# Diagonal attention on one core: rows of queries and keys turned by DMA transposes instead of TensorE transposes and bank copies

## What is computed

```python
Q = X_embed @ W_q + b_q
K = X_embed @ W_k + b_k
V = X_embed @ W_v + b_v
Q = (Q * scale).reshape(n, heads, l, d)      # 16 heads of 8 channels
K = (K * scale).reshape(n, heads, l, d)
V = V.reshape(n, heads, l, d)
scores = jnp.einsum('neax,nebx->neab', Q, K)
A = jax.nn.softmax(scores, axis=2)           # over the query axis
diag = jnp.diagonal(A, axis1=2, axis2=3)
out = (diag[..., None] * V).reshape(n, l, hid) @ W_o + b_o
```

## Time and profile before

| | before |
|---|---|
| median of three runs | 4593.46 us |
| the profiled execution's own time | 4590.25 us |
| its span | 4588.9 us |
| granted TensorE clock over the span | 0.81 of 2.4 GHz |
| busy: PE, PEld, DVE, ACT, POOL | 81%, 43%, 74%, 65%, 19% |
| phase F, first score to the close of the last tile | about 2502 to 3824 us |

### The profile page before, as it was taken

How to read it: one execution, slowest core, us unless ns; L and a number is a source line. 1 busy time by engine, 2 the same in 40 slices (tenths; PEclk the granted TensorE clock), 3 DMA queues, 4 the chain that set the end, 5 groups by cost and what they waited for, 6 DMA issues and landing times.

```text
span 4588.9 us, 77986 instructions
## 1 busy us (share of the span) xinstructions
PE 3731.4 (81%) x30870; PEld 1964.0 (43%) x30870; DVE 3378.4 (74%) x5283; ACT 2974.1 (65%) x4944; POOL 875.9 (19%) x1122
## 2 busy tenths in 40 slices
PE   6999778888599999899997566666666567899998
PEld 4666523232244445666665111111111113566666
DVE  6778676676320116777886999999999996778787
ACT  3655346656343435566665999999998996566665
POOL 2444301000076760000001122221122110000000
PEclk8999769989699999999998555555555558899999
DMA  1000000000311100000000000000000000000000
GB/s 46 1 1 1 3 0 1 1 1 1 89 33 41 37 12 20 7 10 11 2 2 8 1 0 1 1 1 1 1 1 1 5 1 19 6 11 4 9 2 20
DMA packets 51785, 47.38 MB, mean 10 GB/s; under 512 B 21827, under 2 KB 35790, under 8 KB 51406
## 3 DMA queue, kind: packets, MB, share of 16 engines
q1 hardware_dynamic: 51422, 42.39, 3.8%
HBM read 31.75 MB, written 2.23 MB: 7 GB/s over the span
## 4 chain that ended last, share of the span: by engine, by line
PE 43%; DVE 29%; issue 10%; ACT 7%; DMA 0%; POOL 0%; SPq 0%; DVEq 0%; ACTq 0%; POOLq 0%
DVE d_negmax L2728 14%; PE psum L2245 6%; PE psum L2274 6%; DVE f_m_E L2344 6%; PE psum L2260 5%; PE psum L1906 5%; PE psum L1929 5%; ACT d_junk L2793 3%; PE psum L1302 2%; PE psum L1291 2%; PE psum L1270 2%; DVE f_pT_E L2363 2%; DVE wl_negmax L1408 1%; ACT wl_p L1543 1%; PE psum L2651 1%
## 5 line engine op out<-in xcount | busy, mean ns | idle before, releaser
L2728 DVE TENSOR_REDUCE d_negmax<-psum 128x1 f32<-128x1024 f32 x1024 | 1183.5, 1212 | 57.1 <-PE psum L2651 56.0
L2793 ACT ACTIVATE d_junk<-psum,d_negmax 128x1024 bf16<-128x1024 f32 x1024 | 1136.4, 1118 | 108.3 <-DVE d_negmax L2728 100.4
L2651 PE MATMUL psum<-d_qT,d_kT 64*128 64x512 bf16 x2048 | 606.2, 601 | 487.6 <-ACT d_junk L2793 472.5
L2438 ACT ACTIVATE hidden<-psum,f_nm_E 128x1024 f32<-128x1024 f32 x512 | 566.4, 1113 | 144.3 <-DVE f_nm_E L2347 144.1
L2344 DVE TENSOR_REDUCE f_m_E<-psum 128x1 f32<-128x1024 f32 x512 | 601.8, 1217 | 47.4 <-PE psum L2245 46.2
L2245 PE MATMUL psum<-f_k_E,f_q_swapped_E 64*128 64x512 f32 x1024 | 526.5, 624 | 6.5 <-ACT hidden L2438 6.5
L2245 PE MATMUL psum<-f_k_E,f_q_E 64*128 64x512 f32 x1024 | 526.1, 623 | 3.2 <-DMA f_q_swapped_E<-f_q_E 1.2
L2445 ACT COPY f_pT_E<-psum 128x512 f32<-128x512 f32 x512 | 300.0, 586 | 321.3 <-PE psum L2260 321.2
L2274 PE MATMUL psum<-f_pT_E,f_v_E 128*64 128x128 f32 x8192 | 505.4, 276 | 2.5 <-DVE residual L2374 2.5
L2651 PEld LDWEIGHTS psum<-d_qT,d_kT 64*128 64x128 bf16 x2048 | 105.7, 101 | 925.7 <-ACT d_junk L2793 877.5
L2363 DVE COPY f_pT_E<-psum 128x512 f32<-128x512 f32 x512 | 351.4, 686 | 160.9 <-PE psum L2260 151.4
(11 more groups left out here) (344 smaller groups left out, 4945.5 us busy)
## 6 DMA issues: line engine op xcount, KB each, us to landing
moe_gates_on_all<-moe_gate_spill SPq DMA_DIRECT2D x8, 2048.0 KB, 14.1
f_q_swapped_E<-f_q_E SPq DMA_DIRECT2D x64, 128.0 KB, 2.3
moe_w<-in_moe_w SPq DMA_DIRECT2D x8, 256.0 KB, 4.3
out<-residual SPq DMA_DIRECT2D x1, 2048.0 KB, 8.7
residual<-in_hidden_states SPq DMA_DIRECT2D x2, 768.0 KB, 7.4
residual<-in_hidden_states SPq DMA_DIRECT2D x2, 256.0 KB, 3.1
m_taps<-in_m_conv SPq DMA_DIRECT2D x4, 128.0 KB
level_sums<-in_c_sums SPq DMA_DIRECT2D x1, 512.0 KB
```

Of the source, the lines that this page charges most:

```text
L2438: A.activation(pb[:, u % 2, f * 2 * BANK:(f + 1) * 2 * BANK], two(2 * f), ACT.Exp, bias=nm[:, u % 4:u % 4 + 1], scale=SC, accum_out=rs[:, ...
L2651: last = T.matmul(bank(2 + 2 * (at % 3) + jj), kT[half, s, jb * P:(jb + 1) * P], qT[half, s, hf * BANK:(hf + 1) * BANK], start=True, stop= ...
L2728: V.tensor_reduce(mh[:, t % 2, n // 2, n % 2:n % 2 + 1], two(2 + 2 * (at % 3)), X, ALU.max, negate=True).then_inc(*maxed.up(at))
L2793: A.activation(junk[:, at % 3, :], two(2 + 2 * (at % 3)), ACT.Exp, bias=mh[:, t % 2, n // 2, n % 2:n % 2 + 1], accum_out=sh[:, t % 2, n // ...
```

## The change

The three groups of transposes on PE, DVE's two copies and ACT's copy out of the side banks go. In their place SP issues two DMA transposes for each tile, from SBUF to SBUF: `d_q_rows` (128 x 1024 bf16, 256 KB) to `d_qT`, and `d_k_rows` (128 x 2048 bf16, 512 KB) to `d_kT`. A block of 128 x 128 now holds two sets of 64 rows: for the queries the two halves of the tile, for the keys the same keys twice. So `uq` keeps its size in another order, `uk` is twice as large, and POOL writes each with six copies in place of three. The keys' transpose waits for that of the queries to land; both wait for the spread copies, for the transposes of the tile before, and for the last use of the buffers that they overwrite. The loads of the chosen heads (`fr.sp_heads(0)`) now stand on SP behind the transposes of tile 30.

```diff
-                uq = sb(st, "d_q_rows", [P, 2, NH, len(TERMS), HD], BF16)
-                uk = sb(st, "d_k_rows", [P, 2, NH, len(TERMS), HD], BF16)
+                uq = sb(st, "d_q_rows", [P, 2, NH // 2, 2, len(TERMS), HD], BF16)
+                uk = sb(st, "d_k_rows", [P, 2, NH, 2, len(TERMS), HD], BF16)
...
-                    if t + 1 < R:
-                        side += [("rows", t + 1, k) for k in range(3)]
...
+                def sp_rows(t):
+
+                    s = t % 2
+                    for spread, rows, done, u, dst in ((q_spread, q_rows, q_turned, uq, qT), (k_spread, k_rows, k_turned, uk, kT)):
+                        SP.wait_ge(*spread(t))
+                        if t >= 2:
+                            SP.wait_ge(*scored((t - 1) * STEPS - 1))
+                        if t:
+                            SP.wait_ge(*q_rows(t - 1))
+                            SP.wait_ge(*k_rows(t - 1))
+                        if done is k_turned:
+                            SP.wait_ge(*q_rows(t))
+                        SP.dma_start_transpose(dst[:, s, :].rearrange("p (h n) -> p h n", n=P),
+                                               u[:, s].rearrange("p h r n x -> p (h r n x)")).then_inc(*done.one())
...
-                    fr.sp_heads(0)
+                    for t in tl:
+                        sp_rows(t)
+                        if t == R - 2:
+                            fr.sp_heads(0)
...
-                    for _ in range(14):
-                        yield
-                    T.wait_ge(*q_spread(t))
-                    for k in range(3):
...
-                                last = T.transpose(rows[ROWS * r:ROWS * r + ROWS, q * P:(q + 1) * P],
-                                                   u[:, s, eighth].rearrange("p n x -> p (n x)"), identb[:, :])
...
+                    yield
...
-                            T.wait_ge(*row_act(t))
-                            T.wait_ge(*row_dve(t, 1))
+                            T.wait_ge(*q_rows(t))
+                            T.wait_ge(*k_rows(t))
...
-                        V.tensor_copy(dst, bank(side_bank("rows", t, k)).bitcast(BF16)).then_inc(*row_dve.up(t, k))
...
-                    A.copy(kT[:, s, 8 * P:16 * P], bank(side_bank("rows", t, 2)).bitcast(BF16)).then_inc(*row_act.up(t))
...
-                        G.wait_ge(*turned(t - 2, 2))
+                        G.wait_ge(*q_rows(t - 2))
+                        G.wait_ge(*k_rows(t - 2))
                     for g in range(3):
-                        rows = uk[:, s, :, of_k[g], :]
-                        last = G.tensor_copy(rows, wide(heads(part[:, g, HID:2 * HID]), 2, rows.shape[2]))
-                        if g < 2:
-                            gstep(last)
+                        for r in range(2):
+                            rows = uk[:, s, :, r, of_k[g], :]
+                            last = G.tensor_copy(rows, wide(heads(part[:, g, HID:2 * HID]), 2, rows.shape[2]))
```

More of the change, by code:

```diff
@@ L2535, in phase_F @@
                 k_spread = signal("diag_k_spread", tl)
-                turned = signal("rows_turned", [(t, k) for t in tl for k in range(3)])
-                row_dve = signal("diag_rows_dve", [(t, k) for t in tl for k in range(2)])
-                row_act = signal("diag_rows_act", tl)
+                q_turned, k_turned = loads("diag_q_turned"), loads("diag_k_turned")
+                q_before, k_before = q_turned.count, k_turned.count
+                q_rows = lambda t: (q_turned.sem, q_before + 16 * (t + 1))
+                k_rows = lambda t: (k_turned.sem, k_before + 16 * (t + 1))
                 scored = signal("scored", range(R * STEPS))
@@ L2714, in dve_prep @@
                     V.tensor_tensor(vf[:, t % 3, :], bank(bk)[:, 2 * HID:3 * HID], bias[:, 2, :], ALU.add).then_inc(*biased.up(t))
[L2715 to L2720, removed]
-                        V.tensor_copy(dst, bank(side_bank("rows", t, k)).bitcast(BF16)).then_inc(*row_dve.up(t, k))
-                        for _ in range(3):
-                            yield
                 def dve_score(t, n):
@@ L2832, in pool_prep @@
                     if t >= 2:
-                        G.wait_ge(*turned(t - 2, 2))
+                        G.wait_ge(*q_rows(t - 2))
+                        G.wait_ge(*k_rows(t - 2))
                     for g in range(3):
-                        rows = uq[:, s, :, of_q[g], :]
-                        last = G.tensor_copy(rows, wide(heads(part[:, g, 0:HID]), 2, rows.shape[2]))
-                        if g < 2:
-                            gstep(last)
+                        for r in range(2):
+                            rows = uq[:, s, :, r, of_q[g], :]
+                            last = G.tensor_copy(rows, wide(heads(part[:, g, HID // 2 * r:HID // 2 * (r + 1)]), 2, rows.shape[2]))
                     last.then_inc(*q_spread.up(t))
```

## The result

The changed kernel takes 4545.44 us (median of four executions, 4544.77 to 4546.03) against 4593.4 us before; the ratio is 0.9894, with a 95% interval of 0.9877 to 0.9911, that is a gain of 1.1%, between 0.9 and 1.2%. The prediction said 4546.

A forecast was written before the change was run, and what follows sets the result against it. DVE was taken to bound phase F, ACT close behind. Saving 1.76 us in 31 tiles (54.6) and losing 6.7 at the start gave 4542.4 us profiled, 4546 us for the median, 1.0% less; range 4530 to 4680 us.

The forecast's parts named there:

- The bound: In phase F DVE's maxima set the pace, busy 1259 of 1318.7 us, with ACT close behind at 1209.
- DVE's copies, 1.20 us a tile, in full on the path: Two DVE copies for each tile (L2721) go, taking 0.60 us each, 1.20 us a tile, off the path.
- ACT's copy and its stall of 0.56 us: ACT's one copy a tile goes, and with it DVE's whole 0.56 us stall waiting for PE's scores behind it.
- PE's 48 transposes at nothing: Removing PE's 48 transposes for each tile gains nothing, as they lie beside the scores in PE's idle time.
- Period 38.64 us: Time of one phase F tile falls from 40.40 by 1.76 to 38.64 us; 54.6 us over 31 tiles.
- The spread on POOL: POOL's copies of queries and keys grow from 1.53 us each to 2.0 and 3.1, hidden in POOL's 21 us wait.
- the cover: Time from the queries' spread to the next tile's first scores, in which both DMA transposes can hide: 21.8 us.
- D: Time from the queries' spread to the keys' landing, two DMA transposes in turn: 11 us, between 7.2 and 15.
- The start: The first tile has no cover, so its first scores begin later: 6.7 us lost, between 3 and 11.
- The sum: Profiled execution: 4590.25 - 54.6 + 6.7 = 4542.4 us; for the median 4545.6, given as 4546 us.
- Rival 1: Transposes outlast their cover from D = 21.8 us, each us over making 31 tiles 1 us longer; slower, 24 in 100.
- Clock: In phase F the granted TensorE clock, 0.51, stays at its lower level of 1.2 GHz without PE's transposes.

The follow-up runs named there:

- the runs with four and six transposes: Changed kernel with the keys' transpose issued four or six times in each tile, each after the one before landed: 4557.65 and 4766.44 us.

## Why the prediction was right, point by point

- **The bound.** DVE's maxima paced the phase and pace it still, at 1.13 to 1.14 us each.
- **DVE's copies, 1.20 us a tile, in full on the path.** Right: 1.23 measured alone.
- **ACT's copy and its stall of 0.56 us.** Right: 0.62 measured alone. An engine that is not the bound cost the bound time, since the ring of three pairs had some 0.2 us of slack (the prediction's estimate) against a copy of 0.89.
- **PE's 48 transposes at nothing.** Right: 32 of them were kept in a kernel without the stall, 16 in the other, and the two gains together leave nothing for the transposes.
- **Period 38.64 us.** Measured 38.55 in one tile. The F times give 55.5 us over 31 tiles, 1.79 each, in place of 54.6 and 1.76.
- **The spread on POOL.** The queries' six copies took 1.68 us, for the 2.0 assumed, the keys' 2.54 for 3.1; the queries' spread ends 16.5 us after the first scores (16.8 assumed), and the cover is 22.05 us (21.8).
- **D.** The step that was mis-sized. I took 11 us between 7.2 and 15; it is 7.7. The piece of 256 bytes was right by the count of packets. The landings of 3.1 and 4.3 us, with 0.3 us of handing over, lie close to the lower end, 7.2 us, but by two errors that cancel. Eight more blocks cost 1.2 us, so by the medians the moving part of all 24 blocks is 3.6 us and not 2.6, and the fixed part 1.9 us for each transfer and not 2.3. The mean over the whole span was a bad neighbour: its packets are three times as large. The estimate of near 7.6 us from the Trainium skill ("DMA: Bandwidth & Descriptors", section "Latency and other measured facts") agrees with 7.7, though it too had the fixed part too long and the moving part, 3 us, too short; that of 31.4 us, from 1309 ns for each of 24 blocks ("VectorE: DVE Perf Modes", section "The three transpose paths"), does not: eight more blocks made the landing 1.2 us later, 0.15 us a block. As a price for one block alone that figure may well hold; no run here shows one.
- **The start.** Hence 2.8 us lost in place of 6.7: from SP's first load to the first scores 18.28 us before (2484.00 to 2502.28) and 21.04 after (2493.86 to 2514.90). Of the 3.9 us between forecast and measurement, 3.3 are D; the rest is that the queries' spread came no later after the load than before.
- **The sum.** -54.6 + 6.7 = -47.9 was forecast; phase F gives -55.5 + 2.8 = -52.7. The profiled executions differ by only 44.2 us (4590.25 and 4546.03), because the phases ahead of F took 9.9 us longer in the changed kernel's trace (2493.86 for 2484.00); those behind it took 1.3 us less, which the forecast had not. The change's own effect is thus -54.0 us. The medians differ by 48.0. In the last group of runs the gap was 4601.87 - 4547.99 = 53.9 us. So the forecast gain was some 6 us too small (3.9 of it at the start), and the scatter of other phases happened to cover that: the 4546 is luck by this much. Where the 9.9 us arise the granted clock was 0.64 against 0.83; what sets it was not tried.
- **Rival 1** did not come, and was the right thing to fear: its point of decision, 21.8 us, was met from both sides by the runs with four and six transposes. One size in it was off: it let the gain vanish at D = 23.6 us, where the periods are equal again, but the first tile loses D as well, so by its own terms the gain ends at about 23.0 us.
- **Clock.** At 0.52 in the phase, as against 0.51: without the transposes PE stays at its lower level, as assumed.

## What to carry to other kernels

When an engine off the bound does a copy in a ring of few buffers, hold the copy's length against the slack of one turn of the ring; if it is longer, the bound pays for it, here 0.6 us of a copy of 0.89. Hidden work is free up to its cover and costs its full excess in each round beyond it, so measure both the work and the cover, here 7.7 against 22 us. And look at what an in-order engine waits for, not only how long its work is: a matmul moved one step later took away a stall that had looked like the matmul's own length.

## What the runs showed of the hardware

- A DMA transpose from SBUF to SBUF landed after 3.1 us for 8 blocks of 128 x 128 in bf16 and 4.3 us for 16; the difference, 256 KB in 1.2 us, is about 218 GB/s (worked out; the medians are given to 0.1 us, so 200 to 240).
- It holds SP for 1.23 us (8 blocks) and 1.90 us (16 blocks; 1.69 to 2.90) in issuing, by the medians of 32 each; a plain DMA on the same queue took 0.35.
- It moves packets of 256 bytes, whose time comes to 21.6 ns each (0.108 x 16 x 980 us / 78400), where plain loads in small packets had 13.4.
- Four times the keys' transposes, a DMA share of 0.31 in place of 0.11, left DVE's, ACT's and POOL's busy time as it was (1217.9, 1180.3 and 308.9 us against 1217.6, 1180.1 and 309.4).
- The same stretch of an untouched phase, 640 to 700 us, ran at a granted TensorE clock of 0.83 in one execution and 0.64 in another, with 27 and 21 row maxima done in it; the phase ended 9.8 us later.
